# Linear attention and a routed feed-forward layer in one kernel: from unit 14 a down product waits for the sum of the unit just ahead of it

## The reference, cut to what matters

```
xn   = layernorm(x)
combine = route(xn, gate_weight)                 # T x 16, four entries of a row are not zero
up   = einsum('th,ehi->eti', xn, expert_up)      # 256 -> 128 for each expert
down = einsum('eti,eih->eth', silu(up), expert_down)   # 128 -> 256
moe_out = einsum('te,eth->th', combine, down)
shared  = silu(xn @ shared_up) @ shared_down
out  = x + attention(xn) + moe_out + shared
```

## Time and profile before

| | |
|---|---|
| three runs | 950.6, 952.01 and 943.65 us; median 950.6 us |
| the profiled execution | 957.69 us, its span 956.0 us |
| busy share of the span | PE 81%, DVE 73%, ACT 58%, GpSimd 60% |
| granted TensorE clock, mean over the span | 0.911 of full speed |
| instructions | 19692 |

### The profile page before, as it was taken

The page is one execution under the profiler, slowest core; times in us unless marked ns, Lnnn a source line. Parts: engine busy times, 40 slices in busy tenths (PEclk is TensorE's granted clock), DMA queues, the critical chain, the costliest instruction groups (busy, mean ns, idle before and its releaser), DMA issues.

```text
span 956.0 us, 19692 instructions
## 1 busy us (share of the span) xinstructions
PE 776.1 (81%) x5280; PEld 723.1 (76%) x5280; DVE 694.3 (73%) x2411; ACT 556.4 (58%) x1172; POOL 578.1 (60%) x581
## 2 busy tenths in 40 slices
PE   9999999999999999996476777676776777876762
PEld 8898989898898988886376777666776766766761
DVE  7988898888888898898365666655565665665662
ACT  6777777767677766662265555445454554554440
POOL 1167776666667776667455556555656556656554
PEclk9999999999999999998698798988798799787795
DMA  5334554455444333333397888788788878888692
GB/s 186 115 141 170 190 188 182 178 189 189 152 165 172 143 135 119 120 114 123 112 360 222 278 257 264 245 283 251 239 263 257 264 232 277 263 272 260 210 304 59
DMA packets 137564, 194.64 MB, mean 204 GB/s; under 512 B 16608, under 2 KB 113008, under 8 KB 137456
## 3 DMA queue, kind: packets, MB, share of 16 engines
q1 hardware_dynamic: 106640, 108.69, 38.4%
q0 software_dynamic: 28064, 81.93, 22.3%
q10 hardware_dynamic: 2752, 2.77, 1.0%
HBM read 104.19 MB, written 105.04 MB: 219 GB/s over the span
## 4 chain that ended last, share of the span: by engine, by line
PE 56%; DVE 12%; another core or an unknown queue 12%; issue 11%; ACT 4%; POOL 2%; SPq 1%; DMA 1%; ACTq 1%; DVEq 0%; POOLq 0%
PE bank_a L330 20%; PE bank_y L330 15%; PE bank_x L330 14%; PE bank_a L1627 4%; DVE xn L1141 2%; DVE xt_l L1354 1%; ACT xt_h L776 1%; PE bank_a L1452 1%; DVE xn L1372 1%; PE bank_y L1434 1%; POOL rows_by_expert L554 1%; DVE hs_l L1396 1%; ACT hs_h L819 1%; ACT k_l_p L788 1%
## 5 line engine op out<-in xcount | busy, mean ns | idle before, releaser
L554 POOL DMA_INDIRECT rows_by_expert<-xn,slots_now x192 | 197.7, 1030 | 120.1 <-PE bank_a L330 57.9
L1354 DVE TENSOR_TENSOR xt_l<-bank_a,xt_h 128x512 fp32r<-128x512 f32 x143 | 98.4, 688 | 126.1 <-ACT xt_h L776 113.3
L643 POOL DMA_INDIRECT rows_by_expert<-xn,f_id x128 | 123.1, 961 | 91.8 <-issue 29.0
L330 PE MATMUL bank_y<-we,hs_h 128*128 x572 | 137.9, 335 | 33.7 <-DVE xn L1372 8.4
L330 PEld LDWEIGHTS bank_y<-we,hs_h 128*128 128x128 f32 x572 | 102.3, 218 | 44.1 <-issue 43.2
L814 ACT ACTIVATE hid<-bank_x 128x256 f32<-128x256 f32 x143 | 55.4, 387 | 134.6 <-PE bank_x L330 71.4
L776 ACT CAST xt_h<-bank_a 128x512 fp32r<-128x512 f32 x143 | 83.8, 587 | 84.8 <-remote 56.5
L330 PE MATMUL bank_x<-xt_h,k_l_p 128*128 128x256 f32 x284 | 74.7, 323 | 54.6 <-DVE xt_l L1354 19.2
L330 PE MATMUL bank_x<-xt_h,k_h 128*128 128x256 f32 x288 | 74.7, 319 | 34.8 <-DVE xt_l L1354 21.4
L330 PEld LDWEIGHTS bank_x<-xt_h,k_l_p 128*128 128x128 f32 x284 | 57.9, 225 | 57.8 <-DVE xt_l L1354 35.0
L560 POOL DMA_INDIRECT rows_by_expert<-xn,slots_now x64 | 79.8, 1247 | 30.2 <-issue 13.8
(11 more groups left out here) (311 smaller groups left out, 2460.9 us busy)
## 6 DMA issues: line engine op xcount, KB each, us to landing
xn<-rows_by_expert SPq DMA_DIRECT2D x132, 272.0 KB
x_in<-rows_by_expert SPq DMA_DIRECT2D x80, 272.0 KB
rows_by_expert<-spare SPq DMA_DIRECT2D x22, 544.0 KB
out_dram<-rows_by_expert SPq DMA_DIRECT2D x16, 512.0 KB
x_in<-in_L_attn_x_dram SPq DMA_DIRECT2D x15, 512.0 KB
k_f<-rows_by_expert SPq DMA_DIRECT2D x16, 272.0 KB
q_f<-rows_by_expert SPq DMA_DIRECT2D x16, 272.0 KB
spare<-rows_by_expert SPq DMA_DIRECT2D x16, 272.0 KB
```

The costliest lines, as they stand in the source:

```text
L330: last = nc.tensor.matmul(dst, a, b, start=start and k == 0, stop=stop and k == n - 1, skip_group_check=mixed)
L554: G.indirect_dma_start(out=half_rows[:, :], in_=xn[:, c % NB, s, 0:RW], in_offset=None, out_offset=bass.IndirectOffsetOnAxis(ap=slots_now[ ...
L643: G.indirect_dma_start(out=half_rows[:, :], in_=f_y[u % YB][:, tile], in_offset=None, out_offset=offset).then_inc(added[u % CLS], 16)
L1354: V.tensor_tensor(f_l[u % 4], A[u % AB][:, :].rearrange("p (c s t) -> p c s t", c=KD, s=2), f_h[u % 4].bitcast(F32), ALU.subtract).then_in ...
```

## The change: the wait of the down product

From unit 14 the down product of unit `v` waits for `y_ready >= v`, in place of `v - 1`: VectorE must have made the sum of unit `v - 1`, in place of that of unit `v - 2`. Units 0 to 13 are as before. No instruction is added, removed or moved, and the two halves of `bank_y` are used as before.

```diff
@@ -1637,7 +1637,7 @@
                 expert = expert_from(experts, v)
                 moving = [we[:, bass.ds(expert, 1), i, UPW:].rearrange("p o d -> p (o d)") for i in range(2)]
                 pe.wait_ge(fh_lo, v + 1)
-                wait(pe, y_ready, v - 1)
+                wait(pe, y_ready, v - 1 if v < FROM else v)
                 if v == 0:
                     pe.wait_ge(y_summed, B)
                 for tile in range(2):
```

## The result

The kernel after takes 977.5 us (median of 4 runs, 973.4 to 980.6) where the kernel before takes 951.3 in the same job: ratio 1.029, interval 1.024 to 1.033. Forecast were 974 us. The profiled execution of after has 980.57 us (span 978.8), that of before 957.69 (span 956.0), so the two traces differ by 22.9 us, about as the medians do (26.2).

The account below looks back on a forecast made before the run. GpSimd's scatters, with holes from held TensorE reports, bound the kernel at 3.25 us a unit. The waits themselves and the clock cost nothing, shorter runs +23 us: 950.6 + 23 = 974 us, range 938 to 1000.

Parts of the forecast that it names:

- The bound: Units, 525 to 935 us: GpSimd's scatters with the holes between their runs set the pace, 3.25 us a unit.
- The price of the cover: GpSimd's two scatters of a unit without holes: 2 x (0.96 + 0.30) = 2.52 us, meant to hide the new waits.
- The hold: TensorE's reports, from about 2 us into a run of scatters, are held until 1.1 to 1.4 us after its last scatter.
- Does it bind, and for what by itself: TensorE's wait binds for 127 of 129 down products; alternating with VectorE at 2.45 us, hidden under 2.52, costs nothing.
- a cover gone: Without GpSimd's scatters to hide them, TensorE's waits would cost up to (2.45 - 1.86) x 126 = 74 us.
- Through the hold: Held reports leave one banked down product, not two: runs of two units, one in four of one unit (4.1 us); +23 us.
- The clock: TensorE's granted clock: short stops added, long ones shortened, costed at nothing; by the skill's rule alone the change would be slower.
- Hidden wholly: Rival, chance 0.20: GpSimd's scatters cover the new waits, runs keep their mix; 950 us, 941 to 960.
- Faster: Rival, chance 0.18: TensorE's reports beside the scatters are held less often; 905 us, or 858 with no idle time left.
- Much slower: Rival, chance 0.05: every run of scatters has one unit, +107 us, 1058 us.
- All four signs: Mean scatter run below two units; none of six; down products' idle time "<- DVE L1372" above 50 us; 126 units about 433 us.
- the fifth: Sign in GpSimd's timeline: more holes of about 2 us between runs of scatters.

Follow-up runs that it names:

- b_near: Kernel before with SyncE's four waited-for values of a unit masked ahead of its waits, four register operations more: 831.5 us, ratio 1.001 to the kernel before.
- b_pace: b_base with two small GpSimd memsets behind each scatter from unit 14: 1017.0 us, ratio 1.225 to the kernel before.
- a_near: b_near plus the change, TensorE's stricter wait: 844.6 us, ratio 1.016 to the kernel before.
- b_fd3: b_base with GpSimd's first scatter of a unit waiting for one more down product from unit 14: 918.7 us, ratio 1.106 to the kernel before.
- b_reach: b_near with GpSimd's first scatter of a unit waiting for one more down product from unit 14: 841.3 us, ratio 1.011 to the kernel before.
- b_base: Kernel before with waited-for table entries read as the low 16 bits of each 32-bit word: 897.3 us, ratio 1.080 to the kernel before.
- b_same: Kernel before with waited-for table entries in their own table of adjacent 16-bit words: 899.1 us, ratio 1.081 to the kernel before.

## Why the prediction came out right, and what in it did not

**The bound.** GpSimd's scatters set the pace. That holds in both kinds of job: 3.25 us for a unit with holes, 2.55 without. The price of the cover, 2 x (0.96 + 0.30) = 2.52, is close to what b_near runs at, and in b_pace two thirds of what is added to GpSimd is added to the kernel. But the step was incomplete: SyncE's queue stood close behind, with 32 us of waiting in 400. It did not yet delay the units (0.8 us of waiting of TensorE for loaded rows), but had little to spare. Its rows were read for the two loads issued in a run, and their 0.7 us were seen and not asked about.

**The hold.** In the trace of before it is as told: ScalarE and VectorE have 34 idle times of over 1 us between 525 and 935 us that end with "remote", and 32 of these end in a hole, 1.0 to 1.7 us after the last scatter. In after there are 20, 15 of them in a hole, 0.5 to 1.1 us after it; in b_near there is none. That a run of scatters alone is the cause has fallen, since 234 scatters in a row hold nothing in b_near. What differs between the jobs is not shown. It isn't a property of the program: the same kernel before has both times. Nor is it confined to the units: their first up product is at 475 us in before and at 445 in b_near.

**Does it bind, and for what by itself.** It binds, 54.8 us of waiting "<- DVE L1372" in place of 20.0. "Hidden at no cost under 2.52 us" was nearly right: a_near gives it alone, 13.2 us in place of 0, of the 74 that stood for a cover gone. At 2.45 under 2.52 a unit has 0.07 us to spare, so that a late load, as I read it, turns into time that isn't caught up; no run tests this apart.

**Through the hold.** This is the step that carried the forecast. Runs of six are gone, as was said, and runs of one unit are there. But two terms of the sum were wrong. Of 85 runs 38 are of one unit: nearly every second run, not one in four; that alone would have been +42 us by the sum. And a run of one unit with its hole takes 3.67 us in the mean, not 4.1 (the one shown, 4.55, is a long one). The sum also had no runs of three scatters; there are 21, at 4.83 us with their hole. A hole is shorter than the 1.8 to 2.2 us of before, 1.51 in the mean. I take it that a short run often ends before reports are held, so that its hole is the bare way from sum over down product to scatter; the "remote" waits that became fewer fit this, but it was not tested apart. The errors cancel: 3.46 us for a unit against 3.43 in the forecast, 433 us for 125 units against 433 for 126. The direction and the mechanism were worked out; that the number came within 4 us is luck.

**The clock** was costed at nothing: 0.89 against 0.86 in the stretch, so a loss by the clock is ruled out. The prediction added that by the rule of the Trainium skill ("TensorE: Matmul & The Clock Gate", on how oscillation bites in real kernels) alone the change would be slower still. That doesn't follow: the Trainium skill warns there of long idle gaps, such as waits for a load. Between 525 and 935 us after has more stops of TensorE (95 of over 0.15 us, against 46), but those of 1 us or more are 37 in both and shorter in sum, 94.9 us against 105.9. The higher clock does not contradict that.

**The rivals.** "Hidden wholly" names what the jobs without holds come near to, but with 1.6% it isn't wholly hidden there either. "Faster" did not come. Its price for a kernel without holds, 858 us, was of the right kind: before takes 831 in the jobs where nothing is held, and 30 us of its gain lie ahead of the units (their first up product is at 445 us and not at 475). "Much slower" did not come.

**What would show it.** All four signs came: mean run below two units (2.8 scatters in one against 4.2, by the counts above), none of six, 54.8 us of "<- DVE L1372", and 433 us. Of the fifth, "holes of about 2 us", the number rose but not the size.

How the 26 us split is not shown. The wait costs 13 us without holds; if that part is the same with them, the other half goes with the holds, and between units 14 and 118 it is 5.4 of 17.0 us. That the loss of the second banked product is the reason was not separated from the rest in a job with holds; the experiment meant for it (b_fd3, b_reach) ran in jobs without. None of the variants beat the kernel before.

## What to carry to other kernels

Ask of every queue, the DMA issuing one too, how much waiting it has left, before you say which engine sets the pace: the one with the second least hides your change or pays for it. A cover of 2.52 us over 2.45 hides the mean and not the late ones, so cost such a step above nothing. And a step read off one trace, such as what holds reports, is a property of that run until a second one shows it.

## What the runs showed of the hardware that was not expected

- One kernel, the same chip: 961 us in one job, 831 in another. Where the kernel was slow (trace of before), TensorE's reports came late in runs of scatters, and 61 of 411 register and move operations of SyncE took over 0.3 us, mostly 0.7 in place of 0.03; where it was fast (trace of b_near) 0 of 990 did. The cause stays open.
- SyncE loads eight 32-bit table words into registers in 0.53 us (median in before), eight 16-bit words in 2.0 (b_base, b_same), next to each other or not. Four such loads in eight units made a kernel 8% slower.
- Four register operations and two semaphore instructions more for a unit on SyncE's queue: 27 us (ratio 1.026) where its instructions are stretched; four operations alone where they are not: 0.1%, which is no difference.
